# Where ScalarE asks for the table set of Ln and Exp: behind the last gelu of a unit, or behind the first row half's deviation

## The reference

```
k    = conv7x7_dilated2(x, w1) + b1 ;  k = conv1x1(k, w2) + b2     # 49 logits for each pixel
attn = softmax(k over the 49 taps)
x    = sum over the 49 taps of attn * shifted x
y    = gelu(yc[channel, column] + x * D[channel])                  # yc: a small linear scan
out  = x + y
mu, var over the 256 channels of each pixel
out  = (out - mu) * rsqrt(var + 1e-5) * ln_w + ln_b
```

## Time and profile before

| | |
|---|---|
| median of 3 runs | 809.07 us (807.93 to 809.59) |
| span of the profiled execution, first to last instruction | 807.6 us |
| TensorE matmuls | 746.6 us busy, 92% |
| VectorE | 672.8 us busy, 83% |
| ScalarE | 562.8 us busy, 70% |
| GpSimd | 194.6 us busy, 24% |

### The profile page before, as it was taken

One profiled execution on the slowest core, in us unless ns is written; L12 is line 12 of the kernel. 1 busy time (PEld: TensorE's weight loads), 2 busy tenths in 40 slices (PEclk: granted clock), 3 DMA queues, 4 the chain that ended last, 5 costly groups with the idle time before them and its releaser, 6 DMA issues.

```text
span 807.6 us, 27610 instructions
## 1 busy us (share of the span) xinstructions
PE 746.6 (92%) x12338; PEld 446.8 (55%) x12338; DVE 672.8 (83%) x867; ACT 562.8 (70%) x917; POOL 194.6 (24%) x115
## 2 busy tenths in 40 slices
PE   4969989998999999999999999999999999998994
PEld 2535544674557545764567545664567545764581
DVE  0898997988888988988888988988888988686775
ACT  2774454767786796867786696778786687488466
POOL 5114123024211243024211342114311441013011
PEclk9969999999999999999999999999999999999998
DMA  9472233023724147224704245324704230413124
GB/s 293 134 134 38 41 58 50 3 41 52 141 35 93 28 77 122 53 44 75 143 9 94 40 91 95 69 35 87 131 3 93 41 80 3 89 29 70 28 54 105
DMA packets 266721, 58.60 MB, mean 73 GB/s; under 512 B 266265, under 2 KB 266346, under 8 KB 266346
## 3 DMA queue, kind: packets, MB, share of 16 engines
q1 hardware_dynamic: 138488, 40.79, 23.9%
q10 hardware_dynamic: 128114, 16.04, 12.8%
HBM read 40.04 MB, written 16.78 MB: 70 GB/s over the span
## 4 chain that ended last, share of the span: by engine, by line
PE 35%; ACT 22%; DVE 16%; issue 9%; POOL 3%; ACTq 2%; DVEq 0%; POOLq 0%
PE cv L526 18%; PE wk L575 7%; ACT V L913 5%; ACT chs L967 4%; DVE V L1435 3%; PE wk L596 3%; PE wk L634 3%; POOL chs L411 2%; PE ms L606 2%; ACTq L957 2%; DVE o L1583 2%; ACT ms L1016 1%; DVE Z L1476 1%; DVE XT L1466 1%; DVE chs L1535 1%
## 5 line engine op out<-in xcount | busy, mean ns | idle before, releaser
L526 PE MATMUL cv<-V,W 128*32 128x496 f16 (+6 forms) x7840 | 428.9, 374 | 6.3 <-issue 4.1
L526 PEld LDWEIGHTS cv<-V,W 128*32 128x32 f16 (+1 forms) x7840 | 198.5, 96 | 204.8 <-issue 18.2
L913 ACT ACTIVATE V<-R,sc 128x1024 f16<-128x1024 f32 (+1 forms) x88 | 109.6, 1274 | 60.6 <-DVE R L1361 50.5
L386 POOL TENSOR_TENSOR R<-raw 128x1152 f32<-128x1152 f32 x32 | 95.2, 2976 | 201.5 <-DVE V L1435 102.4
L1435 DVE SCALAR_TENSOR_TENSOR V<-R,sc,V 128x1024 f16<-128x1024 f32 (+1 forms) x88 | 115.1, 1327 | 3.0 <-ACT V L913 3.0
L596 PE MATMUL wk<-band,XT 128*128 128x209 f16 (+1 forms) x1080 | 87.7, 238 | 3.3 <-ACT o L989 3.0
L596 PEld LDWEIGHTS wk<-band,XT 128*128 128x128 f16 x1080 | 78.7, 97 | 15.0 <-ACT o L989 8.5
L575 PEld LDWEIGHTS wk<-AT,sel 128*128 128x128 f16 x2268 | 69.6, 100 | 15.0 <-issue 8.6
L411 POOL TENSOR_TENSOR chs<-o 128x1024 f32<-128x1024 f32 x14 | 45.2, 3226 | 130.8 <-DVE o L1583 121.8
L575 PE MATMUL wk<-AT,sel 128*128 128x16 f16 (+1 forms) x2268 | 73.9, 190 | 0.1
L1361 DVE SCALAR_TENSOR_TENSOR R<-R 128x1024 f32<-128x1024 f32 (+1 forms) x56 | 68.6, 1257 | 0.0
(11 more groups left out here) (196 smaller groups left out, 931.1 us busy)
## 6 DMA issues: line engine op xcount, KB each, us to landing
raw<-in_x_dram SPq DMA_DIRECT2D x16, 1024.0 KB, 11.7
out_dram<-o SPq DMA_DIRECT2D x28, 512.0 KB, 4.3
AT<-in_x_dram ACTq DMA_DIRECT2D x82, 128.0 KB, 3.1
w1raw<-in_L_conv_w_dram SPq DMA_DIRECT2D x2, 3136.0 KB, 16.9
xs<-in_x_dram ACTq DMA_DIRECT2D x40, 128.0 KB, 3.0
out_dram<-o SPq DMA_DIRECT2D x8, 256.0 KB, 3.8
AT<-in_x_dram SPq DMA_DIRECT2D x4, 128.0 KB, 3.0
xs<-in_x_dram SPq DMA_DIRECT2D x2, 128.0 KB, 3.7
```

The lines of the kernel that those rows point to most:

```text
L386: nc.gpsimd.tensor_tensor(R[buffer][:, :, :, :], rows_of(par, j + 2), rows_of(par, j), ALU.subtract).then_inc(pool_rows, 1)
L526: ins = pe.matmul(to.rearrange("p (w t c) -> p w t c", w=2, c=COLS)[:, :, :, c0:c1], W[:, ws, h * K7 + v, k0:k1], slot(n, a)[:, low, :, t0 ...
L913: nc.scalar.activation(v_array(n, a, 0), array(a), ACT.Identity, scale=sc[:, par, 3:4]).then_inc(vhi, 1)
```

## The change

ScalarE's request for the set `natural_log_exp_and_others` moves up in its list: from behind `spread_mean(m, 1)` to directly behind `gelu(m, 1, 1)`. It then stands ahead of the squares and of the Ln and Exp of the first row half. Nothing else is edited.

```
@@ scalar engine, unit(n, par) @@
                 attended(m, other, 7)
                 spread_mean(m, 0)
                 gelu(m, 1, 1)
+                table_of_ln()
                 turned_x(n, par, 0)
                 fetch_rows(n, 3)
                 square(m, 0, 0)
...
                 turned_x(n, par, 4)
                 fetch_rows(n, 7)
                 spread_mean(m, 1)
-                table_of_ln()
                 turned_x(n, par, 5)
                 square(m, 1, 0)
                 square(m, 1, 1)
```

## The result

| | before | changed |
|---|---|---|
| median | 809.26 us (807.93 to 810.74, 5 runs) | 800.93 us (799.94 to 802.99, 5 runs) |
| ratio | | 0.9891 [0.9872, 0.9910] |
| profiled execution: span | 807.6 us | 797.8 us |

The changed kernel is faster by 1.09%, 8.8 us (7.3 to 10.4). Predicted were 799.2 us, in a range of 797.0 to 803.0, and a span of 797.7 us. A pass takes 88.0 us (passes 1 and 2, from one first mean to the next; 88.0 were forecast) instead of 90.2 and 89.4.

A forecast was written before the change was run, and what follows sets the result against it. TensorE, 92% busy, was taken as the bound, so only its waits could be won: its 9.9 us mean wait off the 807.6 us span gives 797.7, plus 1.5 for the median, 799.2 us; range 797.0 to 803.0.

The forecast's parts named there:

- The second load: Table load between Ln and Exp of the first row half; removing it saves 1.28 us per pass, wholly on the chain.
- The first load: Table load ahead of that Ln; removing it starts Ln 0.38 us earlier in pass 2, 1.11 us in pass 1.
- The added load: New load behind the last gelu, costing 1.40 us, hidden in ScalarE's idle time before the first square; taken as nothing.
- The removed load at L1005: Load behind the second mean's copies; removal taken as nothing, with ends of 0 and 0.4 us for the last pass.
- The whole wait: TensorE's second-half mean waiting for VectorE's normalise, 9.9 us in 7 waits, would vanish wholly.
- I find no chain that stays in place: Between the second mean and the next pass everything shifts with TensorE, so none of the 9.9 us is given back.
- TensorE's clock, 1.5 us either way: The stretch at 1.2 GHz behind pass 7 could go away or move within the tail: 1.5 us either way.
- From span to median: The median before was 1.5 us above the profiled span; this was left as is, turning 797.7 into 799.2 us.
- The held requests: Rival: transfer requests wait behind the added load on ScalarE, costing about 2.5 us, giving 801.7 us; chance 0.12.
- the slower outcome: Rival: a held request is long in every pass, losing 0.3 us in each, giving about 811 us; chance 0.05.
- A load that holds longer than its record: Rival: the added load takes 2.5 us of a 1.63 us gap, losing 6 us, giving 805 us; chance 0.04.
- The loads did not come back: Rival: the compiler reinserts loads ahead of Ln or Exp; 805.7 us if one stays, no gain if both; chance 0.05.

The follow-up runs named there:

- e4: Changed kernel with the set asked for again between Ln and first Exp of the first row half: 806.38 us, ratio 0.9949 to the kernel before.
- e10: Kernel before, set request in its old place, with the loop's tile-row requests issued by SyncE instead of ScalarE: 805.92 us, ratio 0.9945.
- e5: Changed kernel with two loads, of two sets, behind the last gelu instead of one: 814.97 us, ratio 1.0065 to the kernel before.
- e2: Changed kernel with the set also requested behind the second half's mean copies, its old place: 799.44 us, ratio 0.9870 to the kernel before.
- e1: The changed kernel run again without any edit: 801.67 us, ratio 0.9894 to the kernel before.
- e6: Changed kernel with gelu's set asked for early, ahead of the requests for the first three tiles: 801.32 us, ratio 0.9874 to the kernel before.
- e9: Changed kernel with the loop's tile-row requests issued by SyncE instead of ScalarE: 798.61 us, ratio 0.9859 to the kernel before.
- e11: Changed kernel with tile-row requests on SyncE and gelu's set asked for early: 795.96 us, ratio 0.9829 to the kernel before.
- e3: Changed kernel with the set requested directly ahead of the first half's Ln instead of behind the last gelu: 802.51 us, ratio 0.9902 to the kernel before.

## Why the prediction was right, and where it was off

**The second load, wholly on the chain: right.** 0.69 us from Ln to Exp, and e4 puts the load back alone and gets 1.0 us of wait in each pass back. Its worth is 1.1 us in a pass (7.5 us in e4, 7.6 in e10), since TensorE has some 0.2 us of slack there.

**The first load, 0.38 us in pass 2 and 1.11 in pass 1: right in size.** The Ln now begins 0.05 us after the variance ends, as taken. The prediction rightly read the idle ahead of the load as the issue of the requests, but didn't conclude that the whole price of the load comes from them; e10 shows it: without them the load costs next to nothing.

**The added load, hidden: right.** The gap before the first square fell by 1.43 us in pass 2 (1.63 to 0.20), against 1.40 worked out, and the variance wasn't late. The margin is thin: pass 7 has 0.02 us of it left. e5 shows that the cover is what it rests on. There the price of lost cover was set too low: a us that overruns the gap was paid not once but also through GpSimd's longer add (0.38 us in most passes, 2.2 in pass 3) and, in two of seven passes, through TensorE's lower clock.

**The removed load at L1005, nothing: right** (e2; 0.3 us in pass 7).

**The whole wait goes, 9.9 us: right at its place.** The stretch is 10.3 us shorter.

**"I find no chain that stays in place": this failed, for 1.3 us.** The prediction named a new wait of TensorE in the turns as a sign of being wrong, and there is one, of 0.84 us. Nothing stays in place by the order of the steps, but ScalarE's queue sometimes needs 2 to 3 us for a pair of requests that takes 1.01 as a rule. It is tempting to say that with the wait at L606 gone there is less slack for this. The traces speak against it. Behind the deviation ScalarE next waits for TensorE's second mean, with its copies (L1030). In pass 2 of the kernel before they begin 0.15 us after ScalarE is free, in the changed kernel 0.43 us. ScalarE's timeline before:

```profile
292.86 1.73 ACT L1030 COPY ms<-ms 64x512 f32<-64x512 f32 x3
```

and after:

```profile
288.48 1.74 ACT L1030 COPY ms<-ms 64x512 f32<-64x512 f32 x3 [0.43 <-PE ms L606]
```

And e4, which has the wait at L606 back, loses the 0.8 us of e1 at the same place (60.13 us from the last variance of pass 1 to the first mean of pass 2, against 59.35 before). The kernel before has long requests as well: 11 of its 112 for tile rows in the loop take over 0.95 us each, and 13 of them after. So the loss is better read as what a long request costs this kernel in either form when it falls at a bad place; that the change brings it is not shown. The intervals leave this open too: the gain by ratio, 7.3 to 10.4 us, holds both 9.0 and the full 10.3.

**The span of 797.7 us came out as 797.8 by errors that nearly cancel:** 1.3 us given back and 0.2 us lost in the tail, against 0.4 us that the stretch won beyond the 9.9 and 0.95 us won by start-up, which has nothing to do with the change. That the two agree to 0.1 us is luck; that some 9 us are won is not.

**TensorE's clock, 1.5 us either way: it moved, at little cost.** The part at the lower clock behind pass 7 is still there, one step later: the variance takes 1.08 us instead of the 1.98 of the earlier trace rows, and the second group of turned logits 1.92 instead of 1.04. The granted clock is 0.79 over 736 to 742 us and 0.92 over 742 to 748. TensorE's timeline:

```profile
741.06 1.92 PE L830 MATMUL cv<-id,Z 128*128 128x128 f32 x8
```

**From span to median: 1.5 us taken, mis-sized.** Every run of the changed kernel is 2.0 to 2.1 us above its own span (799.94 and 797.8, 800.93 and 798.9, 802.99 and 801.0), and every run of the kernel before that was measured beside e1 to e4 is 2.0 to 2.2 us above its own. The 1.5 us were the median of three runs less the span of one; with 2.0 us added to its 807.6, the profiled execution before would be the slowest of the three, that of 809.59. After the change the profiled one was the fastest of five, 1.0 us below the median. Both put the median above the 799.2.

**The rivals.** The held requests are refuted, and with them the slower outcome that was built on them (e5 and e6: requests within a load). A load that holds longer than its record is refuted: the copy at 274.25 starts 0.01 us after the load at 272.96 has ended, and the Exp in e4 0.01 after its. The Trainium skill ("ScalarE: Activation LUTs", section "What ACT_TABLE_LOAD costs") gives a drain of about 1.38 us with each switch; it would have delayed the first square by about 1.2 us, and the trace has 0.20 us of idle left there. The loads did not come back: L1011 and L1016 have none, and e10 against e9 shows what both are worth.

## What to carry to other kernels

Don't count table loads; ask which of them stands between two dependent steps of the chain for which the busiest engine waits, and move that one by name into a gap that is as long as the load (here 1.40 us into 1.45 to 1.84). Then look at what else goes through the queue of that engine: here transfer requests held ScalarE's next step for 1.2 us in one place and 4.1 us in another, and with them on SyncE, which computes nothing, the kernel before is 0.5% faster (e10); for the changed kernel (e9) the gain is within the noise. And compare profiled executions over the stretch between two fixed instructions, since the start-up alone moved the first mean by up to 2 us here.

## What the runs showed of the hardware

A load for a set that is already in is executed again at full length when it is asked for by name at another place (e2, 14 loads of 1283 ns).

VectorE and GpSimd blocked each other, and the start times in the records don't tell which one loses. GpSimd's add took 3.34 us instead of 2.36 when VectorE's record began 0.16 us before its own; VectorE's step took 3.49 us instead of 1.28 in e6, where its record is 0.05 us ahead, but in another pass of e6 and in e11, also 0.05 us ahead, it took 1.29 and the add 3.46 to 3.47. The Trainium skill ("SBUF — State Buffer", section "SBUF: two separate sides") has an exclusive lock for a VectorE step with two inputs in SBUF against a GpSimd step that reads SBUF: the one that starts first holds it for its whole length. The sizes agree within 0.2 us: 1.28 + 2.36 - 0.16 = 3.48 us for the blocked add, 3.34 measured; 0.05 + 2.36 + 1.28 = 3.69 for the blocked VectorE step, 3.49 measured. So a step that comes earlier can make a pass longer: 13.1 instead of 11.2 us from first mean to variance in four passes of e6.

TensorE's clock fell to 1.2 GHz for part of 375 to 380 us in e5, behind an idle time of 3.77 us (0.66 granted), and the matmuls there took 1.97 us instead of 1.08. In pass 5 a wait of 1.77 us was followed by a granted clock of 0.66 over 556 to 561 us; in pass 2 one of 1.76 us was not (1.00 over 284 to 289). So of two waits of the same length one was followed by the lower clock and one was not.

A pair of requests for tile rows on ScalarE's queue takes about 1.0 us as a rule, and 1.7 to 3.1 us at times (e1, e3, e4, e6, pass 6 after the change); a single one took 2.11 us. What makes them long isn't settled.
